# An early-fusion kernel: single filter operations, an early first halo, new order lists, and identity turns on TensorE

## The reference, cut to what matters

```python
for _ in range(10):
    u_nabla = _conv(u[:, None], nabla_w)               # row and column differences
    q = q - TAU * (u_nabla[:, 0] * vf1 + u_nabla[:, 1] * vf0)
    q = jnp.maximum(q, 0.0)
    Tq = _conv(jnp.stack([vf1 * q, vf0 * q], axis=1), div_w)[:, 0]
    u = jax.nn.sigmoid((o - Tq) / EPS)
u1 = (o - Tq) / EPS
```

## Time and profile before

| | us |
|---|---|
| median of 3 runs | 1031.03 (1030.58 to 1034.13) |
| profiled execution | 1034.21 |
| its span | 1032.5 |
| PE busy | 922.9 (89%) |
| DVE busy | 852.1 (83%) |
| ACT busy | 684.6 (66%) |
| POOL busy | 115.7 (11%) |

### The profile page before, as it was taken

The page is one execution under the profiler, slowest core; times in us unless marked ns, Lnnn a source line. Parts: engine busy times, 40 slices in busy tenths (PEclk is TensorE's granted clock), DMA queues, the critical chain, the costliest instruction groups (busy, mean ns, idle before and its releaser), DMA issues.

```text
span 1032.5 us, 18335 instructions
## 1 busy us (share of the span) xinstructions
PE 922.9 (89%) x6832; PEld 700.7 (68%) x6832; DVE 852.1 (83%) x1164; ACT 684.6 (66%) x2221; POOL 115.7 (11%) x147
## 2 busy tenths in 40 slices
PE   3389999989999998999998987989998998999987
PEld 2268777767777776877877864767675766667665
DVE  3799999999999999999999997996898599343442
ACT  2468767876876877876876774666746584765742
POOL 5101011011011011111101111110000000000000
PEclk9679999999999999999999988999998999999998
DMA  7301221031010120010220010000001000000000
GB/s 161 116 11 37 78 59 44 21 118 40 19 45 16 32 89 34 17 46 11 68 77 16 12 36 11 11 21 11 27 16 31 21 22 31 27 26 2 17 1 31
DMA packets 24921, 38.97 MB, mean 38 GB/s; under 512 B 4000, under 2 KB 20608, under 8 KB 23552
## 3 DMA queue, kind: packets, MB, share of 16 engines
q1 hardware_dynamic: 24448, 36.74, 11.4%
q0 software_dynamic: 384, 1.05, 0.6%
HBM read 22.21 MB, written 5.24 MB: 27 GB/s over the span
## 4 chain that ended last, share of the span: by engine, by line
DVE 63%; PE 20%; ACT 8%; issue 5%; DMA 2%; POOL 1%; SPq 1%; POOLq 0%; DVEq 0%; ACTq 0%
DVE neg_max L1635 6%; PE ps_t L838 4%; DVE f L1612 4%; DVE f L1608 4%; DVE f L1600 4%; DVE f L1629 4%; DVE f L1611 4%; DVE f L1607 4%; DVE p L1615 4%; DVE f L1628 4%; DVE p L1618 4%; DVE f L1630 4%; DVE f L1603 3%; PE ps_m L849 3%; DVE f L1623 3%
## 5 line engine op out<-in xcount | busy, mean ns | idle before, releaser
L1039 ACT ACTIVATE prob<-ps_s,neg_max 128x128 f32<-128x128 f32 x512 | 182.2, 396 | 11.3 <-DVE neg_max L1635 11.3
L651 PE MATMUL ps_t<-w,hidT 128*128 128x256 f32 x512 | 125.5, 383 | 0.0
L1039 ACT ACTIVATION_READ_ACCUMULATOR prob<-ps_s,neg_max 128x1 f32 x512 | 121.3, 237 | 0.0
L597 PE MATMUL ps_t<-ident,prob 128*128 128x128 f32 x512 | 83.4, 288 | 29.1 <-ACT prob L1039 25.4
L651 PEld LDWEIGHTS ps_t<-w,hidT 128*128 128x128 f32 x512 | 91.1, 190 | 12.2 <-issue 1.8
L838 PE MATMUL ps_t<-km,w_fc 128*128 128x384 f32 x256 | 97.4, 517 | 1.9 <-ACT km L1233 1.9
L597 PEld LDWEIGHTS ps_t<-ident,prob 128*128 128x128 f32 x512 | 63.0, 147 | 51.7 <-ACT prob L1039 33.4
L1047 ACT ACTIVATE probT<-ps_t 128x512 f32<-128x512 f32 x128 | 78.1, 611 | 21.9 <-PE ps_t L597 10.0
L640 PE MATMUL ps_t<-hT_f,w 128*128 128x256 f32 x256 | 84.4, 488 | 2.7 <-ACT hT_f L1051 2.7
L1635 DVE TENSOR_REDUCE neg_max<-ps_s 128x8 f32<-128x1024 f32 x64 | 77.6, 1212 | 3.1 <-PE ps_s L587 3.1
L640 PEld LDWEIGHTS ps_t<-hT_f,w 128*128 128x128 f32 x256 | 62.5, 252 | 18.1 <-ACT hT_f L1051 6.8
(11 more groups left out here) (172 smaller groups left out, 1997.6 us busy)
## 6 DMA issues: line engine op xcount, KB each, us to landing
w<-in_w SPq DMA_DIRECT2D x8, 1024.0 KB, 5.0
u<-u SPq DMA_DIRECT2D x80, 63.0 KB
p<-p SPq DMA_DIRECT2D x80, 63.0 KB
w_attn<-in_w_attn SPq DMA_DIRECT2D x4, 768.0 KB, 4.7
out<-w SPq DMA_DIRECT2D x7, 384.0 KB, 2.5
o_all<-in_o SPq DMA_DIRECT2D x4, 512.0 KB, 3.8
filtered<-f_out SPq DMA_DIRECT2D x4, 512.0 KB, 3.0
x<-filtered SPq DMA_DIRECT2D x8, 256.0 KB, 2.8
```

What stands on the lines that cost most here:

```text
L597: last = tr(ps_t[:, 1, P * hh:P * hh + P], prob[:, n % 2, 4 * half + hh], ident[:])
L651: last = mm(ps_t[:, 0, D * t:D * t + D], hidT[:, m, P * t:P * t + P], w2[:, m], start=False, stop=(m == MC - 1), skip_group_check=True)
L1039: last = A(prob[:, n % 2, hh], ps_s[n % 2][:, hh], ACT.Exp, scale=-1.0, bias=neg_max[:, n % 2, hh:hh + 1], accum_out=den)
```

## The change

On DVE each filter operation becomes an item of its own (columns_apart, columns_weighed, rows_apart, rows_weighed, advance_columns, advance_rows, flux_rows, flux_cols, divergence_columns, divergence_rows, divergence_both, divergence_out). Each counts up a semaphore of its own, and waits for those of the operations whose results it reads or overwrites; none waits behind itself. The state q now takes the column part first, then the row part; in the first iteration of a pair the memset of q is gone and the first part is a product with -1. On SP the first images are loaded ahead of the q/k/v weights, and the first halo of u comes ahead of the wait for the embeddings. ACT makes the first tanh as its first work. PE gets hold_clock: four transposes of the identity into a part of PSUM that turn_probs overwrites later, twice in every text step, and 40 such transposes ahead of the first step; nothing reads their results. All lists of PE, ACT and DVE, and POOL's in fusion, are reordered, and the last sample has its own list, fuse_end.

```diff
@@ -258,12 +261,20 @@
             sp.dma_start(taps[:, 0:18], d["nabla_w"].partition_broadcast(P)).then_inc(s["l_taps"], 16)
             sp.dma_start(taps[:, 18:36], d["div_w"].partition_broadcast(P)).then_inc(s["l_taps"], 16)
             sp.dma_start(pe[:], d["pe"]).then_inc(s["l_pe"], 16)
-            sp.dma_start(w_attn[:, :, 0:3 * D], d["w_attn"][0][:, :, 0:3 * D]).then_inc(s["l_qkv"], 16)
             load_images = lambda k: sp.dma_start(o_all[:, k], d["o"][2 * k:2 * k + 2].rearrange("b (p r) c -> (b p) r c", r=RPP))
             load_images(0).then_inc(s["l_img"], 16)
+            sp.dma_start(w_attn[:, :, 0:3 * D], d["w_attn"][0][:, :, 0:3 * D]).then_inc(s["l_qkv"], 16)
             for img in range(2):
                 for comp in range(2):
                     sp.dma_start(vf[64 * img:64 * img + 64, comp], d["vf"][comp].rearrange("(p r) c -> p r c", r=RPP)).then_inc(s["l_vf"], 16)
+            def rows_below(it):
+                if it < ITERS * PAIRS:
+                    sp.wait_ge(s["act_tanh"], it + 1)
+                    for at in (0, 64):
+                        sp.dma_start(u[at:at + 63, RPP, 0:IMG], u[at + 1:at + 64, 0, 0:IMG]).then_inc(s["halo_u"], 16)
+
+            sp.wait_ge(s["c_pool"], N_CONST)
+            rows_below(0)
             sp.wait_ge(s["g_emb"], 16 * (B - 2))
             sp.dma_start(w_attn[:, :, 3 * D:4 * D], d["w_attn"][0][:, :, 3 * D:4 * D]).then_inc(s["l_wc"], 16)
             sp.dma_start(cols[:], d["cols"]).then_inc(s["l_vec"], 16)
...
@@ -652,49 +656,58 @@
                 if part == 7:
                     last.then_inc(s["pe_ff2"], 1)
 
+            def hold_clock(k):
+
+                pe_.wait_ge(s["act_pT"], 8 * k)
+                for hh in range(4):
+                    tr(ps_t[:, 1, P * hh:P * hh + P], ident[:], ident[:])
+
             def block_step(a, f, it, its):
                 carry_attn(f)
                 project_out(f)
+                hold_clock(a)
                 scores(a, 0)
                 values(a)
                 turn_ffn(f)
+                hold_clock(a)
+                ff1(f, 0)
+                ff1(f, 1)
                 turn_probs(a, 0, 0)
-                ff1(f, 0)
+                ff1(f, 2)
                 turn_probs(a, 0, 1)
-                ff1(f, 1)
-                ff1(f, 2)
+                ff1(f, 3)
+                scores(a, 1)
+                attend(a, 0)
                 turn_probs(a, 1, 0)
-                attend(a, 0)
-                scores(a, 1)
+                carry_ffn(f)
                 turn_probs(a, 1, 1)
-                ff1(f, 3)
-                carry_ffn(f)
...
                 ff_out(f, 1, range(0, 4))
                 ff_out(f, 2, range(0, 4))
 
             pe_.wait_ge(s["c_pool"], N_CONST)
+            for i in range(40):
+                tr(ps_t[:, 1, P * (i % 4):P * (i % 4) + P], ident[:], ident[:])
             first_step()
...
 
+            act.wait_ge(s["l_img"], 16)
+            first_tanh(0)
             act.wait_ge(s["c_general"], 1)
             with act.If(act.value_load(general[0:1, 0:1], min_val=0, max_val=1) > 0):
...
             def block_step(a, f, it, its):
                 norm_attn(f)
+                values_out(a)
+                ffn_in(f)
                 exps(a, 0, 0)
-                ffn_in(f)
-                values_out(a)
                 exps(a, 0, 1)
+                hidden_out(f, 0)
+                hidden_out(f, 1)
                 probs_out(a, 0, 0)
-                hidden_out(f, 0)
-                probs_out(a, 0, 1)
                 exps(a, 1, 0)
                 exps(a, 1, 1)
-                hidden_out(f, 1)
+                hidden_out(f, 2)
+                probs_out(a, 0, 1)
+                filter_out(it)
                 probs_out(a, 1, 0)
...
-            def differences_across(it):
+            def columns_apart(it):
                 if it == ITERS:
                     dve.wait_ge(s["l_img_rest"], 16 * (PAIRS - 1))
-                if it % ITERS == 0:
-                    tick(dve.memset(q_st, 0.0))
                 dve.wait_ge(s["act_tanh"], it + 1)
-                link(tt(fb, u[:, 0:RPP, 1:], u[:, 0:RPP, 0:IMG], ALU.subtract))
+                tt(fb, u[:, 0:RPP, 1:], u[:, 0:RPP, 0:IMG], ALU.subtract).then_inc(s["u_cols"], 1)
+
+            def columns_weighed(it):
                 if it == 0:
                     dve.wait_ge(s["l_vf"], 64)
-                tick(tt(fb, fb, vf[:, 1], ALU.mult))
-
-            def differences_down(it):
+                dve.wait_ge(s["u_cols"], it + 1)
+                tt(fb, fb, vf[:, 1], ALU.mult).then_inc(s["u_cols_v"], 1)
+
+            def rows_apart(it):
+                dve.wait_ge(s["act_tanh"], it + 1)
                 dve.wait_ge(s["halo_u"], 32 * it + 32)
-                link(tt(fa, u[:, 1:, 0:IMG], u[:, 0:RPP, 0:IMG], ALU.subtract))
-                link(tt(fa, fa, vf[:, 0], ALU.mult))
-
-            def advance(it):
-                link(stt(q_st, q_st, 0.0, fa, ALU.max, ALU.subtract))
-                link(tt(q_st, q_st, fb, ALU.subtract))
+                tt(fa, u[:, 1:, 0:IMG], u[:, 0:RPP, 0:IMG], ALU.subtract).then_inc(s["u_rows"], 1)
+
+            def rows_weighed(it):
+                if it == 0:
+                    dve.wait_ge(s["l_vf"], 64)
+                dve.wait_ge(s["u_rows"], it + 1)
+                tt(fa, fa, vf[:, 0], ALU.mult).then_inc(s["u_rows_v"], 1)
+
+            def advance_columns(it):
+                dve.wait_ge(s["u_cols_v"], it + 1)
+                if it % ITERS == 0:
+                    if it:
+                        dve.wait_ge(s["flux_c"], it)
+                    ts(q_st, fb, -1.0, None, ALU.mult).then_inc(s["q_cols"], 1)
+                else:
+                    dve.wait_ge(s["q_rows"], it)
+                    dve.wait_ge(s["flux_c"], it)
+                    stt(q_st, q_st, 0.0, fb, ALU.max, ALU.subtract).then_inc(s["q_cols"], 1)
+
+            def advance_rows(it):
+                dve.wait_ge(s["u_rows_v"], it + 1)
+                dve.wait_ge(s["q_cols"], it + 1)
+                tt(q_st, q_st, fa, ALU.subtract).then_inc(s["q_rows"], 1)
 
             def flux_rows(it):
+                dve.wait_ge(s["q_rows"], it + 1)
+                if it:
+                    dve.wait_ge(s["div_r"], it)
                 stt(p1[:, 1:], q_st, 0.0, vf[:, 0], ALU.max, ALU.mult).then_inc(s["dve_flux"], 1)
 
             def flux_cols(it):
-                tick(stt(p0[:, :, 1:], q_st, 0.0, vf[:, 1], ALU.max, ALU.mult))
-
-            def divergence_across(it):
-                if chain[0]:
-                    dve.wait_ge(s["chain"], chain[0])
-                tick(tt(fb, p0[:, :, 1:], p0[:, :, 0:IMG], ALU.subtract))
-
-            def divergence(it):
+                dve.wait_ge(s["q_rows"], it + 1)
+                if it:
+                    dve.wait_ge(s["div_c"], it)
+                stt(p0[:, :, 1:], q_st, 0.0, vf[:, 1], ALU.max, ALU.mult).then_inc(s["flux_c"], 1)
+
+            def divergence_columns(it):
+                dve.wait_ge(s["flux_c"], it + 1)
+                dve.wait_ge(s["q_cols"], it + 1)
+                tt(fb, p0[:, :, 1:], p0[:, :, 0:IMG], ALU.subtract).then_inc(s["div_c"], 1)
+
+            def divergence_rows(it):
                 dve.wait_ge(s["dve_flux"], it + 1)
                 dve.wait_ge(s["halo_p"], 32 * it + 32)
-                link(tt(fa, p1[:, 1:], p1[:, 0:RPP], ALU.subtract))
-                link(tt(fa, fa, fb, ALU.add))
+                tt(fa, p1[:, 1:], p1[:, 0:RPP], ALU.subtract).then_inc(s["div_r"], 1)
+
+            def divergence_both(it):
+                dve.wait_ge(s["div_c"], it + 1)
+                dve.wait_ge(s["div_r"], it + 1)
+                tt(fa, fa, fb, ALU.add).then_inc(s["div_rc"], 1)
+
+            def divergence_out(it):
+                dve.wait_ge(s["div_rc"], it + 1)
                 stt(fa, o_all[:, it // ITERS], 4.0, fa, ALU.mult, ALU.subtract).then_inc(s["dve_div"], 1)
 
             def head_max(k, n):
...
@@ -1683,69 +1792,89 @@
                     tick(last) if t == 0 else last.then_inc(s["h_ready"], 1)
 
             def block_step(a, f, it, its):
-                differences_across(it)
+                columns_apart(it)
+                columns_weighed(it)
                 moments_attn(f)
+                rows_apart(it)
+                shift_attn(f)
+                advance_columns(it)
+                rows_weighed(it)
                 head_max(a, 0)
-                shift_attn(f)
-                differences_down(it)
-                advance(it)
+                advance_rows(it)
                 flux_rows(it)
+                flux_cols(it)
                 head_max(a, 1)
-                flux_cols(it)
-                divergence_across(it)
-                divergence(it)
+                divergence_columns(it)
+                divergence_rows(it)
+                divergence_both(it)
+                divergence_out(it)
                 head_max(a, 2)
                 if its > 1:
-                    differences_across(it + 1)
```

(60 more changed lines are left out.)

594 lines of the change are left out of this document (341 added, 253 removed).

## The result

The changed kernel has a median of 1020.06 us (1018.60 to 1021.10), against 1030.8 for the kernel before beside it: ratio 0.9884, 95% interval 0.9865 to 0.9903. So it is faster, by 10.8 us and not by 31, and the time lies above the range of the prediction. The profiled execution took 1018.6 us (span 1016.8).

A forecast was written before the change was run, and what follows sets the result against it. DVE was taken to bound the text part, to about 635 us, and PE the last fusion steps. Savings of 9.3 + 0.5 + 13.5 + 1.3 + 7 = 31.6 us off 1031.0 gave 999.4, say 1000; range 986 to 1017.

The forecast's parts named there:

- part 2: Text steps: DVE's waits between dependent filter operations mostly go, 0.90 us a step, 13.5 us over fifteen steps.
- part 5: New order of text steps: every input of DVE still comes 0.4 us or more ahead; 0 us.
- Part 1: Start: earlier image and halo bring iteration 0's row divergence to 33.3 to 34.2 from 42.98, 9.3 us; forty turns 0.
- Rival B: Start: the flux halo lands well after the weights, so only 2 to 3 us are won; 1007, chance 0.10.
- the links: Text steps: 15 DVE starts 1.26 us, not 1.14, after the one before; the new lists leave 7.
- rival A: Text steps: a wait for the spread reciprocal or u halo replaces DVE's, steps stay near 37.2; 1013, chance 0.13.
- Part 3: First state of a pair: dropping the memset gives 0, the one-input advance 0.45 us three times in text, 1.3 us.
- Part 4: Text steps: the eight turns take 0.9 us of PE, which has idle time, so turns and clock are worth 0.
- Part 6: Fusion: PE is the bound, and DVE freed of waits helps where PE pauses; 7 us, bounds -6 and 15.
- The slow step: Fusion step from 776.75 to 826.79, 50.0 us; with DVE earlier it can come down to the 45.0 mean, 5 us.
- Rivals C and D: Fusion: PE never pauses, 20 us gained, 987, chance 0.08; or every step goes like the 50.0 us one, 1041, 0.06.

The follow-up runs named there:

- experiment 6: The changed kernel without the 40 identity turns ahead of the first text step; 1022.63 us, ratio to before 0.9905.
- e1_max_first: The changed kernel with head_max(a, 0) ahead of the norm's shift in text steps and the row difference behind it; 1009.60 us, ratio to before 0.9783.
- experiment 9: The kernel before with the eight identity turns added to every text step, its own lists otherwise; 1033.58 us, ratio to before 1.0004.
- Experiment 3: The changed kernel with the first sample's turns and values moved later on PE and ACT in the last text step alone; 1016.98 us, ratio to before 0.9860.
- e2_shift_late: The changed kernel with advance_columns ahead of the norm's shift in text steps; 1032.56 us, ratio to before 0.9994.
- e8_start_only: The kernel before with only the start changed: image ahead of the q/k/v weights, tanh first on ACT, u halo right behind; 1029.03 us, ratio 0.9967.
- e5_no_hold: The changed kernel without the eight identity turns of each text step, the 40 at the start kept; 1032.78 us, ratio to before 0.9974.
- e7_max_last: The changed kernel with the edits of both e1_max_first and Experiment 3; 1004.94 us, ratio to before 0.9742.

## Why the prediction was wrong
The step that failed is part 2, and with it the sentence of part 5 that every input of DVE is there 0.4 us or more ahead: the sum has 13.5 us for text steps and no term for POOL, on whose reciprocal root DVE then waited 0.93 us a step.

**What bounds the kernel** was read rightly, DVE in text and PE in the last fusion steps. DVE's busy time fell and PE's idle time did not matter.

**Part 1** held: L1730 started at 33.87, inside the forecast 33.3 to 34.2, and the stage gained 9.25 for 9.3 and 0.5. (The middle of the forecast 33.3 to 34.2 gives 9.2, not 9.3.) One trace flatters it, though, which is luck: the second text step started between 56.3 and 59.3 in the kernels that share this start, by how fast the first projections ran (experiment 6), and alone on the old lists the start gave 6.2. Rival B did not occur. The forty turns gave between nothing and 2.8 us, the bound having been 1.5.

**Part 2** is where it failed. The arithmetic of the links was right: starts 1.13 to 1.14 us apart, and both halos covered but in two steps (the halo of u 1.06 and 0.72 us late in the step from 394.48, that of the fluxes 0.45 at 276.57). The walk of the new list failed at one item, the norm's reciprocal root from POOL: in the old step it was there when head_max had ended, and the prediction says nothing of how long POOL takes. The change puts a DVE operation with two SBUF inputs beside POOL's two small ones, POOL's 0.20 us becomes 1.08, and 0.93 us of idle DVE takes the place of the 0.90 saved. The 13.8 us forecast for fourteen steps were 0.1. It is rival A in form (another wait takes the place, each step stays near 37.2), with a chance of 0.13, but with the wrong candidates: I named the spread reciprocal and the halo and never read POOL's rows. They held the warning, L455 at 1.08 and L447 at 0.20 us on the same shapes. That the time still came out faster, at 1020 and not 1031, is the start and fusion, not the text.

The Trainium skill has the rule that I did not weigh: "SBUF — State Buffer", section "Who interferes with whom", says that DVE and GpSimd share one pair of ports as an exclusive lock, that a DVE operation with two SBUF inputs contends with a GpSimd one that reads SBUF, and that the order of issue decides who is blocked. That the loser is blocked for the other's whole instruction it says of DVE's two-port modes. The traces agree, and show it for two inputs as well: 1.08 us beside L1686, ending 0.05 us behind it, 0.20 where POOL started 0.11 us ahead of L1686 (473.06), and 0.20 beside head_max, which reads PSUM.

The rule that I did weigh, that of the Trainium skill in "VectorE: DVE Perf Modes", section "The DRAIN you can't avoid", is not borne out for these operations: starts 1.26 us apart became 1.14, and in e1_max_first, with no wait for POOL, the fourteen steps are 8.7 us shorter than before, 0.62 a step. A part of that is the shorter advance of part 3.

**Part 3.** The memset was free as said: without it DVE's wait for the tanh of iteration 20 is 1.34 us (394.48), where it was 0.26. The advance with one tensor input took 0.69 us at 589.58, as forecast, and 1.08 at 20.14, with POOL at work beside it. Its 1.3 us can't be told apart in the sum.

**Part 4** was right where it was measured by itself: in the old lists the turns are worth 0 (experiment 9). Its error was to apply the spare time of PE in the old step to the new one. In the old list a wait for ACT stands right behind the first ff1 and takes what the clock gives back; in the new one a second ff1 stands there, and the turns are worth 12.7 us, 6.3 once the wait for POOL is gone. That the second ff1 is what makes the difference is argued from the lists; no run moved it alone. The forecast time was not hurt, since the turns are in the changed kernel; the reason was wrong, and by it I would have called them superfluous.

**Part 5** said 0, with every input of DVE 0.4 us or more ahead. For the ordinary steps that was true apart from POOL and the three late halos. For the last text step, which I had not walked, it cost 5.1 us: PE's waits for the first sample's turns and values. Experiment 3 gave 5.3 of that back in the step, 3.1 in the time.

**Part 6** was right in kind and low by size: 12.6 us in the seven steps and 1.35 in the tail for 7 forecast. The slow step came to 45.5, about the old mean as I said, but for a reason only half mine: with DVE freed and the old lists it comes down only to 48.0. Rivals C and D did not occur.

Together, against the forecast of the profiled execution (1034.2 - 31.6 = 1002.6; measured 1018.6): text 19.8 short (14.8 forecast, 5.0 lost), the first fusion stage 2.5 short, the start 0.5 short, fusion and tail 7 better: 15.9 of the 16.0 us.

What stays open: the first fusion stage with its +2.5 us; where the rest of the start's 6.2 us goes in the median; what the forty turns give on the average; and why the granted clock falls in e2_shift_late in spite of the eight turns.

## What to carry to other kernels
When an order is rewritten, look for every small operation of another engine between two items of the list, and ask what now runs beside it, not only how long it took. If one of the pair is GpSimd on SBUF and the other a VectorE operation with two SBUF inputs, put one there that reads PSUM: here that exchange of two lines was worth 10.5 us. A saving on the bounding engine is only there once its waits are walked in every kind of step, the odd last one too. And slack of another engine belongs to one order: the same turns were worth 0, 6 and 13 us in three orders, and in a fourth they did not hold the clock.

## What the runs showed of the hardware
Not expected: POOL's 128x2 operation went from 0.20 to 1.08 us, the one behind it from 0.69 to 1.56, by what DVE ran beside it; where POOL's started 0.11 us ahead of DVE's it kept its 0.20. A chain of DVE operations of 128x1024 elements lost 0.12 us at each direct dependence, and the order alone took that away. With four identity turns in each of two pauses (0.60 us each time) PE's granted clock was 1.00 in all fourteen steps of the changed kernel and 0.91 to 0.96 in thirteen of fourteen without them, and the first eight products behind the pause took 1.99 us and not 3.52. It is no rule: in e2_shift_late the clock fell to 0.91 with the turns, and in e8_start_only it was 1.00 in twelve of the fourteen steps without them. POOL and DVE slow each other at the start as well: while POOL made its masks, the weighed flux L1714 took 1.54 us at 28.48, against 1.22 in a text step, and the masks took 1.43 to 1.96 us in place of 0.63. And the spread of a kernel's executions differs by its order: 16 us in ten runs of e5_no_hold, 8.7 in twelve of e9_hold_before, 1 in four of e7_max_last.
